# A selective scan on one core: how the rows of C reach all 128 partitions

## The reference, cut to what matters

```
xn    = rms-normalised layernorm(x)
x     = silu(conv4(xn @ in_w.T))                  # 256 channels
delta = softplus(x @ wd1.T @ wd2.T + wd2_b)
Bt    = x @ wb.T ;  Ct = x @ wc.T                 # 16 states each
h[t]  = exp(delta[t] * A) * h[t-1] + delta[t] * x[t] * Bt[t]     # per channel and state
y[t]  = sum over states n of h[t, n] * Ct[t, n]
out   = ((y + x * W_D) * silu(skip)) @ out_w.T
```

## Time and profile before

| | us |
|---|---|
| median of 3 runs (2391.93 to 2398.88) | 2395.92 |
| the profiled execution | 2383.14 |
| its span, first to last instruction | 2381.3 |
| stage 2's scans, first scan to the end of the stage | 540.5 to 1062.3 |
| engines busy over the whole span | PE 78%, DVE 67%, ACT 50%, POOL 40% |

### The profile page before, as it was taken

How to read it: one execution, slowest core, us unless ns; L and a number is a source line. 1 busy time by engine, 2 the same in 40 slices (tenths; PEclk the granted TensorE clock), 3 DMA queues, 4 the chain that set the end, 5 groups by cost and what they waited for, 6 DMA issues and landing times.

```text
span 2381.3 us, 33167 instructions
## 1 busy us (share of the span) xinstructions
PE 1868.1 (78%) x12499; PEld 1224.3 (51%) x12499; DVE 1590.2 (67%) x2101; ACT 1195.2 (50%) x2056; POOL 949.6 (40%) x384
## 2 busy tenths in 40 slices
PE   6999999864435444458799998788898877799999
PEld 5444544642222222237677776555565554577776
DVE  4666664673223433348677777999999999976666
ACT  2355445355223333303445555676767766655554
POOL 2466655112332333321010000888888989910000
PEclk8899999977667777778899999999999999999999
DMA  3121120029998899930000000000000000010000
GB/s 80 23 55 28 28 54 2 11 8 27 29 32 35 37 35 35 36 51 1 30 28 27 27 14 1 1 2 2 1 2 2 28 1 2 15 41 14 27 14 18
DMA packets 39491, 53.85 MB, mean 23 GB/s; under 512 B 6147, under 2 KB 22758, under 8 KB 39334
## 3 DMA queue, kind: packets, MB, share of 16 engines
q1 hardware_dynamic: 38806, 50.69, 25.1%
q10 hardware_dynamic: 528, 1.05, 0.2%
HBM read 21.05 MB, written 1.05 MB: 9 GB/s over the span
## 4 chain that ended last, share of the span: by engine, by line
PE 41%; issue 27%; DVE 16%; POOL 5%; ACT 4%; another core or an unknown queue 3%; DMA 3%; SPq 1%; DVEq 0%; POOLq 0%; ACTq 0%; PEldq 0%
PE ps L46 8%; PE ps L47 7%; PE ps L48 7%; DVE negm L2691 6%; PE ps L532 3%; PE ps L548 2%; PE ps L581 2%; DVE AF L2698 2%; DMA AF<-AF 2%; PE ps L573 2%; POOL hc L1567 1%; POOL AR_plain L2496 1%; PE ps L2520 1%; PE ps L2603 1%
## 5 line engine op out<-in xcount | busy, mean ns | idle before, releaser
L1920 DVE TENSOR_TENSOR_SCAN AF<-AF,ps 128x1024 f32<-128x1024 f32 x64 | 146.1, 2285 | 340.5 <-PE ps L1664 339.1
L2691 DVE TENSOR_REDUCE negm<-ps 128x64 bf16<-128x1024 f32 x256 | 301.7, 1212 | 19.9 <-PE ps L2594 19.8
L2496 POOL TENSOR_TENSOR AR_plain<-AF 128x2048 f32<-128x2048 f32 x64 | 261.7, 4094 | 32.1 <-ACT AF L2647 31.9
L46 PE MATMUL ps<-XH,AR 128*128 128x512 f32 x616 | 254.6, 413 | 14.7 <-DVE XL L251 4.0
L2655 ACT ACTIVATE AF<-ps 128x1024 f32<-128x1024 f32 x192 | 196.3, 1022 | 132.5 <-PE ps L2603 131.1
L755 POOL TENSOR_TENSOR AF<-AF 128x2048 f32<-128x2048 f32 (+3 forms) x52 | 184.7, 3552 | 176.2 <-ACT AF L695 173.4
L47 PE MATMUL ps<-XL,AR 128*128 128x512 f32 x616 | 245.4, 398 | 0.0
L48 PE MATMUL ps<-XH,AR 128*128 128x512 f32 x616 | 245.1, 398 | 0.0
L1804 ACT ACTIVATE AR_plain<-AR_plain,AF 128x256 f32<-128x256 f32 x192 | 80.1, 495 | 299.8 <-PE ps L1664 299.7
L695 ACT ACTIVATE AF<-ps 128x512 f32<-128x512 f32 (+1 forms) x304 | 154.0, 576 | 143.8 <-PE ps L532 68.3
L2603 PE MATMUL ps<-negm,ident_bf 128*128 128x512 bf16 x512 | 161.3, 398 | 80.7 <-DVE negm L2691 80.2
(11 more groups left out here) (329 smaller groups left out, 4465.7 us busy)
## 6 DMA issues: line engine op xcount, KB each, us to landing
AR<-AR SPq DMA_DIRECT2D x96, 128.0 KB, 2.4
AF<-AF SPq DMA_DIRECT2D x16, 512.0 KB, 64.2
AF<-AR_plain SPq DMA_DIRECT2D x16, 512.0 KB, 54.1
AF<-in_L_ffn_Wg_dram SPq DMA_DIRECT2D x21, 256.0 KB, 2.8
AF<-in_L_ffn_Wu_dram SPq DMA_DIRECT2D x21, 256.0 KB, 3.1
AF<-in_L_ffn_Wd_dram SPq DMA_DIRECT2D x21, 256.0 KB, 3.9
AF<-in_L_attn_a_Wq_dram SPq DMA_DIRECT2D x1, 512.0 KB, 4.1
AF<-in_L_attn_a_Wout_dram SPq DMA_DIRECT2D x1, 512.0 KB, 9.2
```

What stands on the lines that cost most here:

```text
L46: pe.matmul(out, ah, bh, start=start, stop=False)
L2496: pool.tensor_tensor(p6[m % 3].rearrange("p (j q i) -> p j q i", j=HJ, i=2), e6[m % 4].rearrange("p (j q i) -> p j q i", j=HJ, i=2), w6i[: ...
L2691: dve.tensor_reduce(negm6[:, j % 4, :], bank(2 * (j % 3), 2).rearrange("p (j q i) -> p q j i", j=HJ, i=2), mybir.AxisListType.XY, ALU.max, ...
```

## The change

SP now works in two steps. `copies(b)` takes the 16 partitions of C of batch b and copies them eight times, to partitions 16e to 16e + 15 for e = 0 to 7, into a new tile `ccs[b]` (64 KB a transfer). Row n then lies on the eight partitions n, n + 16, ..., n + 112. `row(j)` spreads it in 16 transfers: transfer m reads those eight partitions and writes the eight partitions 8m to 8m + 7 of `crow[j % 4]` (32 KB). SP waits for the landing of the copies (`s2_cc`) before the first row that reads them. The order on SP is copies(0), rows 0 to 3, copies(1), rows 4 to 31: 16 + 512 transfers instead of 32.

Beside it, `turn_b(1)` moves ahead of `delta(1)`, DVE's copy of it ahead of the scans, and `delta(1)` uses banks 4, 5, 6, 7. ACT takes the first half of it out before its loop and the second half within its first pass; `collect` of chunk c waits for its own half alone.

```diff
+        ccs = [tp(L), raws[:, 0:L]]
-        Z_BANK = [(0, 1, 2, 3), (6, 7, 4, 5)]
+        Z_BANK = [(0, 1, 2, 3), (4, 5, 6, 7)]
         def s2_load(q, s):
-            for j in range(NJ):
+
+            def copies(b):
+                q.wait_ge(s2_drc, 2 * b + 2)
+                q.wait_ge(s2_conv, EC * (b + 1))
+                for e in range(EG):
+                    q.dma_start(ccs[b][NS * e:NS * e + NS], dtr[b][DT + NS:XB]).then_inc(s2_cc, 16)
+
+            def row(j):
                 b, n = j // NS, j % NS
-                q.wait_ge(s2_drc, 2 * b + 2)
+                q.wait_ge(s2_cc, 16 * EG * (b + 1))
                 wait(q, s2_hc, EC * (j - 3))
-                q.dma_start(crow[j % 4].unsqueeze(1),
-                            dtr[b][DT + NS + n:DT + NS + n + 1, :].unsqueeze(1).to_broadcast([1, P, L])).then_inc(s2_cd[j % 4], 16)
+                for m in range(NS):
+                    q.dma_start(crow[j % 4][EG * m:EG * m + EG], ccs[b][n::NS]).then_inc(s2_cd[j % 4], 16)
+
+            copies(0)
+            for j in range(4):
+                row(j)
+            copies(1)
+            for j in range(4, NJ):
+                row(j)
 # s2_pool
-                pool.wait_ge(s2_cd[j % 4], 16 * (j // 4 + 1))
+                pool.wait_ge(s2_cd[j % 4], 16 * NS * (j // 4 + 1))
 # s2_pe: delta
                 if b:
-                    pe.wait_ge(s2_btc, 1)
+                    pe.wait_ge(s2_btc, 2)
 # turn_b
                 if b:
-                    pe.wait_ge(s2_zc, 4)
+                    pe.wait_ge(s2_drc, 4)
+                    pe.wait_ge(s2_btc, 1)
 # collect
                 if n == 0:
-                    pe.wait_ge(s2_zc, 4)
+                    pe.wait_ge(s2_zc, 2 * c + 2)
                     if b:
                         pe.wait_ge(s2_y2, c + 1)
-                    elif c:
-                        pe.wait_ge(s2_btc, 2)
 # order on PE
             turn_x(0, 1)
+            turn_b(1)
             delta(1)
...
-                if k == 1:
-                    turn_b(1)
 # s2_act
-            for n in range(4):
-                c, i = n // 2, n % 2
-                act.wait_ge(s2_z, 4 + n + 1)
-                act.activation(dl[1][:, c, 512 * i:512 * i + 512], bank(Z_BANK[1][n]), ACT.Identity,
-                               bias=db[:, c:c + 1]).then_inc(s2_zc, 1)
-            act.wait_ge(s2_zc, 4)
+            def take_delta(c):
+                for i in range(2):
+                    n = 2 * c + i
+                    act.wait_ge(s2_z, 4 + n + 1)
+                    act.activation(dl[1][:, c, 512 * i:512 * i + 512], bank(Z_BANK[1][n]), ACT.Identity,
+                                   bias=db[:, c:c + 1]).then_inc(s2_zc, 1)
+
+            take_delta(0)
             for j in range(NJ):
                 if j + 1 < NJ:
                     decay(EC * (j + 1))
+                if j == 0:
+                    take_delta(1)
+                    act.wait_ge(s2_zc, 4)
 # s2_dve: the copy of turn_b(1) now stands before the loop over the scans
```

More of the change, by code:

```diff
@@ L1398, in build @@
         NP = B * EC
+        EG = P // NS
         NJ = B * NS
@@ L1464, in build @@
         s2_drc = sem("s2_drc")
+        s2_cc = sem("s2_cc")
         s2_cd = [sem("s2_cd%d" % i) for i in range(4)]
@@ L1888, in s2_dve @@
                 dve.tensor_tensor(dx[:, c, :], x, xc[0][:, c, :], ALU.mult).then_inc(s2_mul, 1)
+            dve.wait_ge(s2_bt, 2)
+            dve.tensor_copy(bT[1].rearrange("p t n -> p (t n)"), bank(6)[:, 0:LB * NS]).then_inc(s2_btc, 1)
             def inputs_middle(j):
@@ L1921, in s2_dve @@
                                        ALU.mult, ALU.add).then_inc(s2_h, 1)
-                if k == 1:
-                    dve.wait_ge(s2_bt, 2)
-                    dve.tensor_copy(bT[1].rearrange("p t n -> p (t n)"), bank(6)[:, 0:LB * NS]).then_inc(s2_btc, 1)
                 if k % EC == EC - 1 and k // EC + 2 < NJ:
```

## The result

The changed kernel takes 2198.7 us (median of 4 runs, 2194.83 to 2200.36) against 2394.4 for the kernel before on the same chips: ratio 0.918, 95% interval 0.916 to 0.920, 196 us less. The forecast was 2224 (2165 to 2278), 172 us less. The profiled execution has a span of 2198.6.

The account below looks back on a forecast made before the run. Rows of C, read from one partition at 27 GB/s, were taken as the bound at 16.0 us a row. At 10.4 us a row, set by SP's issues, the saving 505 - 32 P is 172 us: 2395.9 - 172 = 2224 us (2165 to 2278).

Parts of the forecast that it names:

- What bounded the kernel: Stage 2: scans wait for rows of C, read from one partition at 27 GB/s, 16.0 us a row.
- Source: Reading each row from eight partitions 16 apart gives 108 GB/s or more, at most 4.9 us a row, no longer a limit.
- Issue on SP: 16 transfers a row at 0.65 us each cost SP 10.4 us a row (8.2 to 11.0).
- The sum: Stage 2 ends at 557.2 + 32 P against 1062.3; saving 505 - 32 P, 172 us.
- P: Time per row of C in the forecast, 10.4 us; the saving is zero at 15.8.
- Destination: Each transfer writes two blocks of four partitions, 0.61 or 0.67 us, 9.7 to 10.7 us a row, beside the issue.
- Engines: POOL and PE need 6.3 to 9.9 us a row, under the 10.4 of SP.
- Small steps: Moving batch 1's small steps is worth zero, covered by the wait for row 1; without cover about 1 us either way.
- A: Rival: SP issues faster, then engines or destination are next; 8.5 to 9.7 us a row, 2163 to 2201 us; 18%.
- C: Rival: transfers don't overlap, 19.4 to 30.4 us a row, 2512 to 2864 us, slower than before; 5%.
- B: Rival: the DMA engines carrying a row limit, 0.75 to 0.91 us a transfer, 2275 to 2358 us; 11%.
- D: Rival: rows were not the limit, something else POOL waits for takes over, no change; 1%.

Follow-up runs that it names:

- Experiment 6: Changed kernel with its 16 transfers of 32 KB a row all read from the one partition that holds row n: 2502.6 us, ratio 1.045 to the kernel before.
- experiment 8: Against experiment 7, every row reads the same eight neighbouring partitions 0 to 7: 2218.2 us, ratio 0.926 to the kernel before.
- experiment 7: Changed kernel with one copy transfer a batch and one 512 KB transfer a row, read from eight neighbouring partitions: 2081.7 us, ratio 0.871 to the kernel before.
- experiment 1: Changed kernel with each row spread by one 512 KB transfer, the eight source partitions each read 16 times: 2076.6 us, ratio 0.869 to the kernel before.
- experiment 5: Changed kernel with transfer m writing partitions m, m + 16, ..., m + 112 instead of eight neighbours: 2195.3 us, ratio 0.918 to the kernel before.
- experiments 9 and 10: Halves of the change: kernel before with only the new spreading of C, 2198.9 us (0.920); changed kernel with the old spreading, 2393.3 us (1.001).
- experiment 12: Against experiment 1, batch 1's small steps stand as in the kernel before: 2082.6 us, ratio 0.870 to the kernel before; partner 2075.6 us.

## Why the prediction was right, and where it was off

**What bounded the kernel.** Right, and shown: the pace of C's rows was set by reading one block of four partitions at 27 GB/s. Experiment 6 keeps the transfers and restores only the source, and 27 GB/s return; experiment 8 gives some 50 for two blocks. The mean of 16.0 us instead of 19.5 was put down to rows in flight in different blocks; experiments 7 and 8 show that effect at work, from 10.5 us a row down to 5.2, where PE takes over. What fell short is that the prediction did not carry this into a rule: it would have said 9.7 us for experiment 7, and so did the expectation.

**Source.** Right: with eight partitions 16 apart it was no limit. With four rows queued, experiment 1 moves 101 GB/s, a row in 5.2 us; the prediction had 108 or more and at most 4.9. That partitions at distance 32 are tied, which it left open, is what the 101 show.

**Issue on SP.** The mechanism was right, and it sets the end: 16 x 0.612 = 9.79 us. The term was mis-sized, 0.65 for 0.612. The nearest rows were of other shapes, 128 KB between 32 partitions or 8 KB from 16 partitions onto one. The issue depends on the shape: its median is 0.497 us from four partitions to four, 0.563 from eight to eight, 0.592 from eight to 16. It does not follow the bytes: 512 KB from eight to 128 partitions take 0.592 to 0.594. A few issues were long (up to 1.218), too few to show in the mean.

**The sum.** Saving = 505 - 32 P was right in form. The 32 rows took SP 313.5 us (531.56 to 571.59, and 577.29, where the chain has row 4's first issue, to 850.71), which makes 191.5. The copies cost 7.0 and 5.7 us, not twice 7.3: 1.9 more. From the last row's start to the end of the stage it took 19.2 us, not 20.9: 1.7 more. The last landing came 1.8 us after the issue, not 2.2. Together 195.5, measured 195.6. So 19 of the 24 us by which the forecast missed are the price of an issue.

**Destination.** The value taken (0.61 us by two blocks) lay beside the issue and so did no harm, but no run supports or refutes it: experiment 5 doubles the blocks or more, and SP's pitch of about 0.61 hides whatever that saves. A destination limit above 54 GB/s into eight neighbours was not tried.

**Engines.** Under 10.4, as said, but 6.3 to 9.9 was too high: the floor is 5.19 us a row. The three steps of 9.43 us had been read right behind an idle stretch, with TensorE at its lower clock at first, as this row of the kernel before shows; the same collect takes 1.89 us in experiment 1.

```profile
855.70 3.78 PE L1678 MATMUL ps<-hc,ident 128*128 128x512 f32 x4 [5.98 <-POOL hc L1567]
```

Between 650 and 740 the granted clock is 1.00 in experiment 1, 0.87 in the changed kernel and 0.66 before.

**Small steps.** Zero as forecast, by experiments 9 and 10. "About 1 us either way" without the cover was too low: 3 us of the stage in experiment 12, and 7 by the medians, which is not certain. The wait of 6.3 us on DVE stood in the trace of before, and only the two PE steps had been priced:

```profile
551.25 0.29 DVE L1924 COPY AF<-ps 128x128 f32<-128x128 f32 x1 [6.28 <-PE ps L1644]
```

**Rivals.** P = 9.8 lies in the gap between A (to 9.7) and the forecast (from 10), nearer to A. Of A the first half came true, an issue cheaper than 0.65; the second did not, since neither the engines nor the destination were next and the issue still set the pace. The pitch of 0.612 us excludes C, whose forms need 1.21 us or more a transfer, and B, which needs 0.75; experiment 1 shows besides that the carriers of a row can move 101 GB/s. D is excluded by the gain itself. Of the Trainium skill's rules, the port rule (SBUF — State Buffer, "The DMA port swizzle") agrees: 27, 50 and 101 GB/s for one, two and four blocks, with the partitions at distance 32 counted as one block. The Trainium skill (SBUF — State Buffer, "Can I just issue two DMAs to hit both halves?") says that two concurrent transfers serialize. The runs differ, and the measurement decides: transfers of 32 KB follow each other every 0.61 us, though the last one of the stage is taken up 1.8 us after its issue ended, and rows in flight together move 131 GB/s in experiment 7, where rows confined to the same two blocks stay at 50.

## What to carry to other kernels

A broadcast from one SBUF partition runs at the rate of one block of four partitions, 27 GB/s, and more carriers don't help: it was 27 at a DMA share of 0.94 in the kernel before and at 0.47 in experiment 6. A share that is high for the GB/s moved is its mark. Spread the source over blocks first; then count issues, since each cost SP 0.5 to 0.6 us here, from 16 to 512 KB, and let one transfer read each source many times: this version, experiment 1, beats the changed kernel by 122 us. Once a long wait is removed, look again at every idle stretch that it covered.

## What had not been expected of the hardware

The issue of a transfer within SBUF depends on its shape and not on its bytes. From four, eight and eight partitions to four, eight and 16 it takes 0.497, 0.563 and 0.592 us, and to 128 partitions about as long as to 16; but one partition read eight times takes at least 0.619, so it is not the number of partitions alone. And rows that are in flight together escape a block's limit to a large part: eight neighbouring sources gave 50 GB/s when all rows read the same ones and up to 131 (560 to 570 in experiment 7) when each row had its own.
